# Cross attention with six context slots, a loop of three pairs and a new order of all engines

## The reference

```python
x = x + xattn(layernorm(x), ctx, ctx, ...)     # q = x1 Wq^T + bq, k = x2 Wk^T + bk, v = x3 Wv^T + bv
                                               # softmax(q k^T) v over 1500 rows, no scale
x = x + ffn(layernorm(x), ...)                 # 16 heads; 8 experts, two chosen for each token and head
return x
```

## Time and profile before

| | |
|---|---|
| median of 3 runs | 509.18 us (507.96 to 509.66) |
| the profiled execution | 509.82 us, its span 508.0 us |
| mean granted TensorE clock | 0.969 of full |
| PE busy in the span | 424.5 us (84%) |
| DVE busy | 428.5 us (84%) |
| ACT busy | 333.6 us (66%) |
| POOL busy | 149.6 us (29%), all of it before 220 us |
| transfers | 29.46 MB |

### The profile page before, as it was taken

How to read it: one execution, slowest core, us unless ns; L and a number is a source line. 1 busy time by engine, 2 the same in 40 slices (tenths; PEclk the granted TensorE clock), 3 DMA queues, 4 the chain that set the end, 5 groups by cost and what they waited for, 6 DMA issues and landing times.

```text
span 508.0 us, 25659 instructions
## 1 busy us (share of the span) xinstructions
PE 424.5 (84%) x10763; PEld 362.0 (71%) x10763; DVE 428.5 (84%) x805; ACT 333.6 (66%) x904; POOL 149.6 (29%) x139
## 2 busy tenths in 40 slices
PE   2749878889898889837799999999999999999875
PEld 2527767777777778736687877878787877887755
DVE  5756999887888888477899999999999999999832
ACT  5446666765767755436578766876687767876661
POOL 6654997776677776200000000000000000000000
PEclk9898999999999999959999999999999999999996
DMA  7934344454334510000000000000000000000000
GB/s 193 295 113 127 128 130 145 157 166 149 124 124 136 173 63 4 2 1 3 3 4 6 5 0 5 5 5 0 5 5 5 5 0 5 5 5 0 8 8 10
DMA packets 18154, 29.46 MB, mean 58 GB/s; under 512 B 3016, under 2 KB 14024, under 8 KB 18120
## 3 DMA queue, kind: packets, MB, share of 16 engines
q1 hardware_dynamic: 18120, 28.97, 18.1%
HBM read 28.05 MB, written 0.92 MB: 57 GB/s over the span
## 4 chain that ended last, share of the span: by engine, by line
DVE 48%; PE 30%; issue 14%; ACT 4%; DVEq 1%; DMA 1%; SPq 1%; POOL 0%; ACTq 0%; POOLq 0%
DVE ctxf_all L947 8%; DVE ctxf_all L921 6%; PE ps L1052 6%; DVE ah L975 3%; DVE attnf L958 3%; DVE ctxT L729 3%; PE ps L1083 3%; PE ps L1279 2%; PE ps L1098 2%; PE ps L1099 2%; PE ps L1100 2%; PE ps L1108 1%; DVE oh L894 1%; DVE eq L873 1%; DVE eq L888 1%
## 5 line engine op out<-in xcount | busy, mean ns | idle before, releaser
L379 POOL TENSOR_TENSOR nat<-ctxf_all,nat 128x640 f16<-128x640 f32 x32 | 67.0, 2110 | 45.4 <-ACT nat L501 45.2
L601 ACT ACTIVATE e_sb<-ps,smn 128x56 f32<-128x56 f32 x256 | 76.2, 369 | 1.9 <-DVE smn L965 1.9
L501 ACT CAST nat<-ctxf_all 128x1536 f16<-128x1536 f32 x32 | 45.8, 1471 | 39.8 <-PE ps L1100 37.7
L1052 PE MATMUL ps<-ident,nat 128*128 128x128 f16 x768 | 61.0, 225 | 11.7 <-DVE ctxT L729 3.4
L601 ACT ACTIVATION_READ_ACCUMULATOR e_sb<-ps,smn 128x1 f32 x256 | 67.0, 268 | 0.0
L1052 PEld LDWEIGHTS ps<-ident,nat 128*128 128x128 f16 x768 | 46.4, 100 | 27.1 <-issue 16.1
L947 DVE TENSOR_TENSOR ctxf_all<-mixp,diag_h 128x3584 f16<-128x3584 f16 x32 | 63.2, 2018 | 0.0
L385 POOL TENSOR_TENSOR p<-pf,p 128x672 f16<-128x672 f32 x32 | 46.1, 1461 | 13.5 <-ACT pf L514 13.5
L1067 PE MATMUL ps<-qk_cur,ctxT 128*128 128x56 f16 x384 | 34.3, 189 | 12.8 <-DVE ctxT L729 10.8
L729 DVE COPY ctxT<-ps 128x1024 f16<-128x1024 f16 x64 | 42.8, 685 | 2.4 <-PE ps L1052 2.4
L506 ACT COPY ctxT<-ps 128x1024 f16<-128x1024 f16 x32 | 33.0, 1033 | 17.9 <-PE ps L1052 17.9
(11 more groups left out here) (169 smaller groups left out, 1256.2 us busy)
## 6 DMA issues: line engine op xcount, KB each, us to landing
ctxf_all<-in_ctx_dram SPq DMA_DIRECT2D x32, 704.0 KB
ctxf_all<-in_ctx_dram SPq DMA_DIRECT2D x32, 46.0 KB
x_all<-in_x_dram SPq DMA_DIRECT2D x4, 224.0 KB
out_dram<-y_all SPq DMA_DIRECT2D x32, 28.0 KB
ctxf_all<-in_ctx_dram SPq DMA_DIRECT2D x32, 18.0 KB
fwq_nat<-in_L_ffn_Wq_dram SPq DMA_DIRECT2D x1, 512.0 KB, 8.6
fwk_nat<-in_L_ffn_Wk_dram SPq DMA_DIRECT2D x1, 512.0 KB, 9.4
fwv_nat<-in_L_ffn_Wv_dram SPq DMA_DIRECT2D x1, 256.0 KB, 5.9
```

Source lines behind the costliest of these rows:

```text
L379: pool.tensor_tensor(nat[k][:, 1, 7 * C:], ctxf[k][:, 7 * C:], nat[k][:, 0, 7 * C:], ALU.subtract).then_inc(natlo2, 1)
L501: act.copy(nat[k][:, 0, :], ctxf[k][:, :]).then_inc(nathi, 1)
L601: last = act.activation(e_sb[:, k, b, 0:S], ps[:, b, S * k:S * k + S], ACT.Exp, bias=smn[:, K16 * b + k:K16 * b + k + 1], scale=-1.0, accu ...
L1052: last = pe.transpose(ps[:, (3 * b + c) % 2, :].bitcast(F16)[:, P * (j % 8):P * (j % 8) + P], nat[k][:, j // TK, C * (j % TK):C * (j % TK) ...
```

## The change

- `ctxf` and `nat` have six buffers (`RING`) instead of four, `qk_cur` three instead of two, and the loops hold three pairs (`DEEP`). The weights of the second stage are loaded behind the first twelve entries.
- `steps` of all engines is replaced by `step`, for one pair with its own new order; values come one step behind the scores as before, the result and the moments two steps behind (three for the copy of the moments).
- The turns of the next pair stand between scores, values and shift; chunk 0 of slot 1 is turned ahead of chunk 2 of slot 0 (`TURNS`).
- `shift` of both slots is one run of eight matmuls, each on the 64 partitions of its slot instead of all 128, alternating between slots; one semaphore step releases both slots.
- ACT writes the f32 exponentials ahead of the f16 ones, casts one entry at the start of a step and one at its end, and has the second context copy between the exponentials of the two slots.
- The copy of the moments into `mv_all` moves from DVE to POOL (`keep_moments`). `x2_all` is gone: `keep` writes into `x_all`, and bias products lie in tiles that the second stage uses later.
- All four groups are normalised on DVE; groups two to four are turned and multiplied during step 0; the bias products and additions of POOL lie around steps 0 to 2.

```diff
+    DEEP = 3
+    RING = 2 * DEEP
...
-        T_BANK, Q_BANK = (2, 3, 6, 6), (6, 7, 7, 7)
+        T_BANK, Q_BANK = (2, 6, 6, 6), (7, 6, 6, 6)
+        TURNS = ((1, 2, 4), (3, 5, 6))
+        TURNS_0 = ((1, 2, 3), (4, 5, 6))
...
+            def keep_moments(pair):                                   # GpSimd
+                after(pool, mvc, pair + 1)
+                pool.tensor_copy(mv_all[:, bass.ds(pair * 2, 2)], mv_cur[:, :]).then_inc(mvd, 1)
...
+            def step(u, s):                                           # GpSimd
+                if has(u - 1):
+                    low_probs(2 * u - 2, 0, u - 1)
+                if has(u - 3):
+                    keep_moments(u - 3)
+                if has(u - 1):
+                    low_probs(2 * u - 1, 1, u - 1)
+                if has(u + 1):
+                    low_rows(2 * u + 3, slot(s, 1, 1))
+                if has(u + 2):
+                    queries(u + 2, (s + 2) % DEEP)
+                    low_rows(2 * u + 4, slot(s, 2, 0))
+                if has(u - 2):
+                    keep(u - 2)
...
+            def exps(b, pair):                                        # ScalarE
+                after(act, shd, 2 * pair + 2)
+                after(act, plo, 2 * pair + b - 1)
+                act.activation(pf[b]..., ACT.Exp).then_inc(expd, 1)
                 after(act, dend, pair)
                 act.activation(p16[:, 0, :, b, 0:S]..., ACT.Exp).then_inc(expd, 1)
...
+            def step(u, s, i):                                        # ScalarE, without what only step 0 has
+                t_evac(2 * u + 2, u + 1, 0)
+                split_hi(2 * u + 4, slot(s, 2, 0), i + (s + 2) // DEEP)
+                exps(0, u)
+                t_evac(2 * u + 3, u + 1, 1)
+                exps(1, u)
+                split_hi(2 * u + 5, slot(s, 2, 1), i + (s + 2) // DEEP)
...
+            def step(u, s):                                           # VectorE, without what only step 0 has
+                tile_max(2 * u, u, 0)
+                result(u - 2)
+                spread(u - 2)
+                tile_max(2 * u + 1, u, 1)
+                t_evac(2 * u + 2, u + 1, 0, 0)
+                shifts(u)
+                split_lo(2 * u + 3, slot(s, 1, 1))
+                t_evac(2 * u + 2, u + 1, 0, 2)
+                moments_ready(u - 2)
+                t_evac(2 * u + 3, u + 1, 1, 0)
+                moments(u - 2)
+                sums_out(u - 1)
+                den_out(u - 1)
+                split_lo(2 * u + 4, slot(s, 2, 0))
+                t_evac(2 * u + 3, u + 1, 1, 2)
...
-            def shift(n, pair, b):
+            def shift(pair):
                 after(pe, dgr, pair + 1)
                 for a in range(2):
-                    o = ps[:, 2 + 2 * b + a, 0:6 * S].rearrange("p (t q) -> p t q", t=6)
                     for part in range(2):
-                        last = pe.matmul(o, rows_of[:, b, :],
-                                         dg[:, part, :].unsqueeze(1).broadcast_to((P, 6, S)),
-                                         start=False, stop=(part == 1), skip_group_check=True)
-                last.then_inc(shd, 1)
+                        for b in range(2):
+                            r = slice(SLOT * b, SLOT * b + SLOT)
+                            o = ps[:, 2 + 2 * b + a, 0:6 * S].rearrange("p (t q) -> p t q", t=6)
+                            last = pe.matmul(o, rows_of[r, b, :], dg[r, part, :].unsqueeze(1).broadcast_to((SLOT, 6, S)),
+                                             start=False, stop=(part == 1), skip_group_check=True)
+                last.then_inc(shd, 2)
...
+            def step(u, s):                                           # TensorE, without what only step 0 has
+                scores(2 * u, u, s, 0)
+                turn(2 * u + 2, 0, slot(s, 1, 0), (0,))
+                scores(2 * u + 1, u, s, 1)
+                turn(2 * u + 2, 0, slot(s, 1, 0), (1,))
+                values(2 * u - 2, u - 1, 0, slot(s, -1, 0))
+                max_turn(u)
+                values(2 * u - 1, u - 1, 1, slot(s, -1, 1))
+                turn(2 * u + 3, 1, slot(s, 1, 1), (0,))
+                turn(2 * u + 2, 0, slot(s, 1, 0), (2,))
+                shift(u)
+                denominator(u - 1)
+                turn(2 * u + 3, 1, slot(s, 1, 1), (1,))
+                turn(2 * u + 3, 1, slot(s, 1, 1), (2,))
+                project(u - 1)
```

More of the change, by code:

```diff
@@ L77, in xattn_ffn @@
         x_all = sb("x_all", [P, NP * C])
-        x2_all = sb("x2_all", [P, NP * C])
         y_all = sb("y_all", [P, NP * C])
@@ L173, in xattn_ffn @@
         d_fw = sem("d_fw")
-        d_ctx = [sem(f"d_ctx{k}") for k in range(4)]
+        d_ctx = [sem(f"d_ctx{k}") for k in range(RING)]
         d_out = sem("d_out")
@@ L285, in xattn_ffn, with has, slot, turned @@
         GC = NP * C // NG
-        T_BANK, Q_BANK = (2, 3, 6, 6), (6, 7, 7, 7)
+        T_BANK, Q_BANK = (2, 6, 6, 6), (7, 6, 6, 6)
+        TURNS = ((1, 2, 4), (3, 5, 6))
+        TURNS_0 = ((1, 2, 3), (4, 5, 6))
+        def has(pair):
+            return not isinstance(pair, int) or 0 <= pair < NP
+        def slot(s, off, b):
+            return 2 * ((s + off) % DEEP) + b
+        def turned(pair, b, c):
+            first = isinstance(pair, int) and pair == 0
+            return 6 * pair + (TURNS_0 if first else TURNS)[b][c]
         GW = B * S // NG
@@ L395, in queries @@
                 if isinstance(pair, int):
-                    pool.wait_ge(qk_lo, pair // 4 + 1)
+                    pool.wait_ge(qk_lo, min(NG, pair // 4 + 1 if pair < 4 else NG))
+                after(pool, qkc, pair)
+                after(pool, st_done, 2 * pair - 2 * DEEP + 2)
                 pool.tensor_copy(qk_cur[s][:, :, :], qk_all[:, :, bass.ds(pair * (2 * S), 2 * S)]).then_inc(qkc, 1)
-            def steps(i):
-                for s in range(2):
-                    pair = 2 * i + s
-                    n = 2 * pair
-                    first = isinstance(pair, int) and pair == 0
-                    more = not (isinstance(pair, int) and pair == NP - 1)
-                    if more:
-                        low_rows(n + 2, (2 * s + 2) % 4)
-                        low_rows(n + 3, (2 * s + 3) % 4)
-                        queries(pair + 1, 1 - s)
-                    low_probs(n, 0, pair)
-                    low_probs(n + 1, 1, pair)
-                    if isinstance(pair, int) and pair < 4:
-                        add_bv(pair)
-                        if pair < 3:
-                            bias_products(pair + 1)
-                    if not first:
-                        keep(pair - 1)
@@ L446, in add_bv @@
                                    bv_all[:, :].unsqueeze(1).broadcast_to((P, 4, C)), ALU.add).then_inc(c_xbv, 1)
+            def step(u, s):
[12 more added lines that the diff above has]
+                    keep(u - 2)
+            bias_products(0)
             low_rows(0, 0)
             low_rows(1, 1)
-            queries(0, 0)
-            apply(2)
-            bias_products(0)
-            apply(3)
-            steps(0)
-            steps(1)
-            with pool.Fori(2, NP // 2 - 1) as i:
-                steps(i)
-            steps(NP // 2 - 1)
-            keep(NP - 1)
+            queries(1, 1)
+            low_rows(2, 2)
+            step(0, 0)
+            bias_products(1)
+            add_bv(0)
+            bias_products(2)
+            step(1, 1)
+            bias_products(3)
+            add_bv(1)
+            step(2, 2)
+            add_bv(2)
+            add_bv(3)
+            with pool.Fori(1, NP // DEEP - 1) as i:
+                for s in range(DEEP):
+                    step(DEEP * i + s, s)
+            for u in range(DEEP * (NP // DEEP - 1), NP + 3):
+                step(u, u % DEEP)
         @block.scalar
@@ L724, in split_lo, with t_evac @@
                                   ALU.subtract).then_inc(natlo, 1)
-            def t_evac(n, b, c):
-                after(dve, tfull, 3 * n + c + 1)
+            def t_evac(n, pair, b, c):
+                after(dve, tfull, turned(pair, b, c))
                 after(dve, st_done, n - 1)
@@ L1162, in _ @@
             x_qk(0)
-            turn(0, 0, 0, (1,))
-            x_turn(1)
-            turn(0, 0, 0, (2,))
-            x_qk(1)
+            turn(0, 0, 0, (1, 2))
             turn(1, 1, 1, (0,))
+            scores(0, 0, 0, 0)
+            turn(1, 1, 1, (1, 2))
             pe.wait_ge(c_zero, 9)
-            steps(0)
-            with pe.Fori(1, NP // 2 - 1) as i:
-                steps(i)
-            steps(NP // 2 - 1)
+            for u in range(DEEP):
+                step(u, u)
+            with pe.Fori(1, NP // DEEP) as i:
+                for s in range(DEEP):
+                    step(DEEP * i + s, s)
+            for u in range(DEEP * (NP // DEEP), NP):
+                step(u, u % DEEP)
             pe.wait_ge(d_fw, 16 * NFW)
```

331 lines of the change are left out of this document (151 added, 180 removed).

## The result

The changed kernel takes 486.34 us (median of four, 485.39 to 487.98) where the kernel before took 509.42 beside it (507.96 to 512.93): a ratio of 0.9541, 95% interval 0.9483 to 0.9598. The profiled execution took 487.15 us with a span of 485.4, where before's had 508.0.

The account below looks back on a forecast made before the run. No engine was full; VectorE's queue plus the holes its order leaves bounded the pair. Pair 15 coming 24.5 us earlier and +0.3 in the tail gave -24.2 us, a median of about 485.0 (481 to 489; 479 to 499 with rivals).

Parts of the forecast that it names:

- The loop: Steady cross-attention pair, from second scores to second scores through shift and exponentials: 8.98 us, where before took 10.83.
- The halves of the rows: Shift's eight matmuls on 64 rows each: halves overlap, issue 0.56 us plus 0.09 for the change of shape.
- the rival's 9.54: Shift: the row halves don't overlap, pair 9.54 us, whole 493; chance 0.29 together with losing one GpSimd-VectorE meeting.
- The three meetings: GpSimd against VectorE at the shifts and both L723 low rows: VectorE first by 0.0, 0.3 and 0.2 us.
- the lost meeting: GpSimd's L385 gets ahead of the second L723: pair 9.7 to 10 us; chance 0.29 together with row halves not overlapping.
- the taken chain: GpSimd operations block VectorE's L742, L746 and L748, delaying the shift: pair 11.3 us, whole 517; chance 0.06.
- The removed copy: VectorE's copy of the moments (L779) with the wait ahead of it: 0.89 us a pair off VectorE's queue.
- The start of pair 1: Pair 1's second scores, after query groups are turned in step 0: near 45.3 us instead of 46.21, between 42 and 49.
- The early pairs: GpSimd's bias products and additions squeezed into steps 0 to 2: 4.5 us above the loop, bounds 2.2 and 9.
- The tail: After the loop, the first shift starts both slots together, so ScalarE starts later: +0.3 us.
- no gain: Holes return as PE waiting for VectorE's copies, pair near 10.8 us, whole 509; chance 0.03 for above 499 to 509.
- better: Neither first pair nor early pairs lose, pair 8.7 us, whole 479; chance 0.10.

Follow-up runs that it names:

- two additions in a gap: Changed kernel with key-bias sums and products early, plus GpSimd's `bv` additions of groups 1 and 2 moved into its idle time in step 1: 481.49 us.
- GpSimd busy in the gap: Changed kernel plus an unused GpSimd addition of 384 columns behind the query copy in the looped pairs: 500.29 us.
- zeros on one half: Changed kernel, shift as slot 0's four matmuls, four more adding zeros on the same rows, then slot 1's four: 492.68 us in one execution.

## Why the prediction was right, step by step

- **The total.** 485.0 was forecast, 479 to 499; it is 486.34. In the loop the mechanism was the one described. That the sum comes within 1.3 us is luck in part: the loop was 2.5 us too long in it and the early pairs 3.8 us too short.
- **The loop, 8.98 forecast, 8.80 measured** (14 x 0.18 = 2.5 us too much). From the start of the second scores: shift at 4.39, as said (4.3 and the change of shape); results at 5.15 forecast, ACT starting at 5.17; its last exponential ending at 8.74 against 8.77. What failed was the hand-over from ACT to PE: 0.2 in the sum, 0.06 in the trace. I had read it off a row that joins two casts, whose first end isn't shown, and off a turn that wasn't waiting. In the trace of before, PE comes to the turn at 117.56 straight from its denominators (24 of them in 0.61 us, up to the row of the turn in the earlier trace rows):

```profile
116.95 0.74 PE L1108 MATMUL ps<-ones,p 128*128 128x1 f16 x24
```

- **The halves of the rows.** 0.56 for the run and 0.09 for the change of shape were booked, the 0.09 without a row for it. Measured: 0.09 ahead of the run, and 0.67 for it, of which about 0.11 is the change back. With all rows the pair is 9.20, not the rival's 9.54: the two changes of shape, 0.09 and 0.11, go away with the overlap, and the hand-over is short there too. The Trainium skill's "TensorEngine Tiling (Array Packing)", Key Properties, says that tiles work in parallel and that a change of mode drains TensorE: the runs agree with the first by the single starts above. The two changes of shape, 0.09 and 0.11 us, fit a drain, but no run here shows what PE does in them.
- **The three meetings.** Forecast for VectorE by 0.0, 0.3 and 0.2 us. Measured: the query copy ends at 110.18, 0.08 after L767 has begun, and L767 isn't stretched; L748 comes 0.28 ahead of L395 and 0.30 ahead of L401. All three go as said, in every steady pair, and the two rivals that hang on them were produced: 9.80 for the lost meeting (9.7 to 10 forecast) by one small copy, 11.2 to 11.4 for the taken chain (11.3 forecast) by an operation of 0.99 us that fills GpSimd's hole of 0.94. The Trainium skill's "SBUF — State Buffer", Who interferes with whom, has it that the order of issue decides who blocks; these runs agree, with 1.07 against 2.23 us for the same L746.
- **The removed copy.** Booked with 0.89 us of VectorE's queue. Alone, in the old order, it brought 0.64. In the new order putting it back costs 0.4 to 1.0 in the loop, the larger where it turns the meeting, and nothing behind it. The brackets of the steady step show PE and ScalarE setting its 8.80, not VectorE, so the 8.7 that this term led to was a bound only.
- **The start of pair 1, 45.3 forecast, 45.98 measured**, well inside 42 to 49.
- **The early pairs, 4.5 forecast, 8.3 measured** (+3.8 us), near the upper bound of 9. This is the step that failed. I spread 2.0, 1.5, 0.5 and 0.5 over four pairs as GpSimd's work; it is 0.1, 4.5, 3.6 and 0. The first of the two large ones goes with VectorE's two key-bias sums, which the changed kernel has in a row between steps 1 and 2, with PE waiting for the result behind them: without the additions it stays (13.31), without the sums it falls to 9.94. GpSimd's part in it is the smaller: it stretches two of these operations, and 1.1 us more go when its additions are moved as well (8.85). The changed kernel's list had the sums in it, and the sum of the prediction had no term for them.
- **The tail, +0.3 forecast:** 307.9 us from pair 15's scores to the end against 308.0, so nothing is seen of it. But a term of 0.3 can't be read from two executions: with the same second stage the other traces here have 303.7 to 309.0.
- **The rivals.** No overlap, taken chain and no gain are each excluded by the 8.80; *better* had the right pair length but not the early pairs. The kernel with two additions in a gap comes near that case: 481.5.

Seen in whole: of the 2.03 us a pair, the row halves hold 0.40 (shown by undoing them). The copy holds up to 1.0, by undoing it, or 0.64, by moving it alone. The rest, 0.6 to 1.0, is left for the new order, the six slots and the longer loop; none of these was tried by itself, and the parts need not add up, since each shifts the meetings.

## What to carry to other kernels

Lay out one turn of the loop as a chain from the event that starts it to the same event of the next turn, and work out the margin of each meeting of two engines at a shared resource: here margins of 0.3 us and a hole of 0.94 us decided between 8.8, 9.8 and 11.3 us a turn. Work that a reordering pushes to the seams between the first turns deserves a row-by-row account of its own, on both engines; moving it into gaps that the trace shows brought 5 us, moving it ahead of the first turn brought nothing. And undo a change part by part before saying which part paid: the copy that was worth 0.89 us by the rows gave 0.64.

## What the runs showed of the hardware

**Two row halves need no alternation.** Four matmuls on one half of the rows, followed by four on the other, take 0.69 us where alternating ones take 0.67, each matmul at its full 0.14: the second four start 13 ns after the first. There is a limit to it: behind eight on one half, the first on the other starts 0.59 us late, when the fifth has started. The change from 128 rows to 64 costs 0.09 us ahead of the run; the change back is what is left of the 0.67, about 0.11.

**The first 45 us and the last 20 differ between executions.** One kernel above (GpSimd busy in the gap) has the same instructions as the changed kernel until just ahead of the loop, yet its pair 1 starts at 47.39 instead of 45.98. Windows of the changed kernel, then of that one (columns as above, clock third from the end):

```profile
25.40:45.00 19.60, 12.44 (x122) 9.32 (x120) 10.57 (x21) 11.10 (x16) 11.35 (x8) 0.76 0.41 136
```

```profile
25.40:45.00 19.60, 11.77 (x103) 7.62 (x100) 11.74 (x20) 10.43 (x14) 11.36 (x8) 0.71 0.35 117
```

And the timeline of the changed kernel, PE, where the granted clock goes up in the midst of a run of scores:

```profile
45.39 0.21 PE L1102 MATMUL ps<-qk_cur,ctxT 128*128 128x56 f16 x1
45.43 0.19 PE L1103 MATMUL ps<-qk_cur,ctxT 128*128 128x56 f16 x1
45.46 0.19 PE L1101 MATMUL ps<-qk_cur,ctxT 128*128 128x56 f16 x1
```

Start to start is about 0.046 us up to there and 0.026 behind: the levels of 1.2 and 2.4 GHz. In the windows of this stretch the granted clock was at the lower level from 40 us on, after PE had been all but idle (0.04 us busy from 38 to 40), and it rose while PE was busy. In the other kernel the whole run of these scores (44.88 to 46.54) passes at 0.047. Of the 1.41 us by which its pair 1 is later, 0.97 is there already when this run starts (43.91 against 44.88). That the clock makes the whole difference isn't shown; but differences of 1 to 2 us between two single executions here say nothing about an edit.

At the end it is more. From the last product with `diag_e` on VectorE to the last instruction the changed kernel takes 21.1 us and the kernel with zeros on one half 16.4, with the same instructions; the granted clock is 0.50 from 478 us to the end in the first, and 1.00 throughout in the second.
